# Attention with normalised queries and keys: two key heads per step on the two halves of 64 rows, queries stored without zero padding

## What is computed

```
q, k, v = xq @ wq, xkv @ wk, xkv @ wv      # 16 query heads, 4 key/value heads, 64 channels each
q, k = a * rsqrt(mean(a*a over the 64) + eps) for a in (q, k)
logits = (q @ k.T) / 8                     # each key head serves 4 query heads
out = softmax(logits) @ v @ wo             # added to the residual
```

## Time and profile before

| | |
|---|---|
| median of 3 runs | 2206.13 us |
| lowest, highest | 2204.80, 2211.46 us |
| the profiled execution's own time | 2202.19 us |
| its span | 2200.4 us |
| PE busy | 1836.1 us, 83% |
| DVE busy | 1396.9 us, 63% |
| ACT busy | 877.2 us, 40% |
| mean granted TensorE clock | 0.915 of full |
| `L2_ca` from its first scores to its last projection | about 1129 to 1390 us |
| `L2_sa`, the same | about 1516 to 1667 us |

### The profile page before, as it was taken

The page is one execution under the profiler, slowest core; times in us unless marked ns, Lnnn a source line. Parts: engine busy times, 40 slices in busy tenths (PEclk is TensorE's granted clock), DMA queues, the critical chain, the costliest instruction groups (busy, mean ns, idle before and its releaser), DMA issues.

```text
span 2200.4 us, 34499 instructions
## 1 busy us (share of the span) xinstructions
PE 1836.1 (83%) x10658; PEld 1321.1 (60%) x10658; DVE 1396.9 (63%) x3343; ACT 877.2 (40%) x2513; POOL 640.2 (29%) x710
## 2 busy tenths in 40 slices
PE   5969997399848779998879998877887779988978
PEld 4747775388736567776745554663445655655557
DVE  5856666111168756666756676676777876777765
ACT  4635553122236425554334443333332354444421
POOL 2235553200033335555300000220002243544433
PEclk9979998599969889999879999888998899999979
DMA  4100000388720000010100200110001000001000
GB/s 162 31 19 15 14 0 1 128 272 301 261 101 1 0 8 16 15 45 5 57 15 15 71 0 1 48 58 1 0 0 68 1 11 11 10 10 37 41 1 17
DMA packets 34247, 102.76 MB, mean 47 GB/s; under 512 B 2624, under 2 KB 25696, under 8 KB 26976
## 3 DMA queue, kind: packets, MB, share of 16 engines
q1 hardware_dynamic: 32608, 97.79, 12.9%
q0 software_dynamic: 1536, 3.67, 0.6%
HBM read 93.20 MB, written 8.26 MB: 46 GB/s over the span
## 4 chain that ended last, share of the span: by engine, by line
PE 60%; DVE 18%; issue 10%; ACT 4%; POOL 4%; DMA 3%; DVEq 0%; SPq 0%; POOLq 0%; ACTq 0%
PE ps L750 9%; PE ps L867 7%; PE ps L710 5%; PE ps L715 5%; PE ps L902 4%; PE ps L813 4%; PE ps L763 4%; PE ps L795 4%; PE ps L745 3%; PE ps L997 2%; POOL arena L1734 2%; PE ps L981 2%; DMA arena<-rows_hbm 2%; PE ps L790 2%; PE ps L702 2%
## 5 line engine op out<-in xcount | busy, mean ns | idle before, releaser
L1734 POOL TENSOR_TENSOR arena<-arena,rinv 112x375 f32<-112x375 f32 (+1 forms) x448 | 371.3, 829 | 563.6 <-DVE rinv L1411 555.6
L750 PE MATMUL ps<-arena 128*112 128x375 f32 (+1 forms) x1280 | 387.7, 411 | 20.0 <-ACT arena L1104 13.0
L763 PEld LDWEIGHTS ps<-cst,arena 112*125 112x125 f32 (+1 forms) x1408 | 216.2, 183 | 157.0 <-POOL arena L1734 55.0
L1104 ACT ACTIVATE arena<-ps,negmax 112x375 f32<-112x375 f32 (+1 forms) x384 | 190.2, 500 | 190.9 <-DVE negmax L1406 189.9
L1406 DVE TENSOR_REDUCE negmax<-ps 112x1 f32<-112x375 f32 (+1 forms) x288 | 159.4, 553 | 161.4 <-PE ps L750 161.1
L763 PE MATMUL ps<-cst,arena 112*125 112x112 f32 (+1 forms) x1408 | 229.2, 275 | 38.2 <-POOL arena L1734 37.9
L750 PEld LDWEIGHTS ps<-arena 128*112 128x112 f32 x1280 | 177.3, 183 | 65.7 <-issue 24.6
L1782 POOL TENSOR_TENSOR w_split_sb<-wml,w_split_sb 128x512 fp32r<-128x512 f32 (+1 forms) x40 | 44.8, 1121 | 575.2 <-ACT w_split_sb L1153 573.3
L1104 ACT ACTIVATE arena<-arena,negmax 112x112 f32<-112x112 f32 (+1 forms) x256 | 125.8, 493 | 171.3 <-DVE negmax L1406 171.2
L1420 DVE COPY arena<-ps 125x336 f32<-125x336 f32 x384 | 187.7, 489 | 2.3 <-PE ps L763 1.7
L867 PE MATMUL ps<-h_split_sb,w_split_sb 128*128 128x448 f32 x768 | 178.0, 381 | 8.3 <-DVE h_split_sb L1531 4.3
(11 more groups left out here) (198 smaller groups left out, 3035.8 us busy)
## 6 DMA issues: line engine op xcount, KB each, us to landing
wml<-in_wm_L_moe SPq DMA_DIRECT2D x21, 1028.0 KB, 5.6
wml<-in_wm_L_moe SPq DMA_DIRECT2D x21, 1024.0 KB, 6.1
craw<-in_ctx SPq DMA_DIRECT2D x40, 375.0 KB
wml<-in_wm_L_m SPq DMA_DIRECT2D x3, 3072.0 KB, 12.9
wat<-in_wa_L_ca SPq DMA_DIRECT2D x2, 2560.0 KB, 9.2
wml<-in_wm_L_m SPq DMA_DIRECT2D x2, 2048.0 KB, 9.6
rows_hbm<-wml SPq DMA_DIRECT2D x2, 1344.0 KB, 14.4
arena<-rows_hbm SPq DMA_DIRECT2D x21, 128.0 KB, 5.6
```

The costliest lines, as they stand in the source:

```text
L750: last = mm(ps[0:S, S_BANK + s % blk.s_banks, i * blk.nk:(i + 1) * blk.nk], qz[:, parity(b), head_of(u) if blk.dh == 16 else u], kT[:, par ...
L763: last = nc.tensor.transpose(ps[0:blk.kp, T_BANK + s % blk.t_banks, o:o + S], buf[:, i * blk.nk + q * blk.kp:i * blk.nk + (q + 1) * blk.kp ...
L1104: last = go(probs[0:S, s % blk.nprobs, i * nk:(i + 1) * nk], src[:, i * nk:(i + 1) * nk], ACT.Exp, bias=negmax[:, u:u + 1], accum_out=rows ...
L1734: pool.tensor_tensor(p3, p3, r3, ALU.mult).then_inc(scaled, 1)
```

## The change

In the two blocks a step's scores are no longer issued one by one. At every even step PE issues the scores of steps s and s+1 together: both use only 64 rows, one rows 0 to 63 (`z` = 0) and the other rows 64 to 127 (`z` = 1), into two banks. For that, the steps of `L2_ca` are renumbered: the two heads of a 128-row tile alternate, so that steps 0 to 5 are chunk 0 of heads 0 and 1, chunk 1 of both, chunk 2 of both. `qz` holds the queries once, without zeros, and ACT empties a QT piece in one pass. DVE's additions follow the new numbering. The tables of steps, pieces and banks are the same.

```diff
@@ scores (PE)
+                    n = 2 if blk.pairs else 1
-                    wait(pe, free, count(base, units, b, s - blk.s_banks + 1))
+                    wait(pe, free, count(base, units, b, s + n - blk.s_banks))
...
+                    if blk.pairs:
+                        for z in range(2):
+                            bank = blk.bank_at(s + z)
+                            if blk.keys_first:
+                                g, q = group_of(blk, s + z)
+                                rows = slice(64 * z, 64 * z + 64)
+                                mm(ps[0:blk.kp, bank, 0:HG * S], kT[rows, parity(b), g // 2, q * blk.kp:(q + 1) * blk.kp],
+                                   qz[rows, parity(b), 4 * (g // 2):4 * (g // 2) + 4], start=True, stop=True).then_inc(scored, 1)
...
+                        return
@@ body (PE)
-                        if b != B:
+                        if b != B and (s % 2 == 0 or not blk.pairs):
                             scores(b, s)
@@ piece (ACT)
+                        if blk.pairs:
+                            last = go(qz[:, par, 4 * i:4 * i + 4], W[:, 0:4 * S].rearrange("p (r s) -> p r s", s=S), ACT.Identity, scale=0.125)
-                        for z in range(2):
+                        for z in range(0 if blk.pairs else 2):
@@ exps (ACT), add_chunks (DVE)
-                        g, q = divmod(s, blk.kc)
+                        g, q = group_of(blk, s)
```

More of the change, by code:

```diff
@@ L87 @@
 }
+PAIRS = ("L2_ca", "L2_sa",)
 class Attn:
@@ L109, in __init__ @@
         self.wg = 1 if dh == 16 else 2
+        self.pairs = name in PAIRS
         self.nprobs = 4
@@ L117, in __init__, with bank_at @@
         self.early = [x for s in sorted(self.plan) if s < self.out_step for x in self.plan[s]]
+    def bank_at(self, s):
+        return (s % 3 if s < 14 else 2 * s - 28) if self.s_banks == 3 else s % self.s_banks
     def in_bank(self, bank, before=None):
@@ L485, in head_of, with place, group_of @@
             return 8 * (u // 8) + 2 * (u % 4) + u // 4 % 2
+        def place(blk, u):
+            return 4 * (u // 4) + (0, 2, 1, 3)[u % 4] if blk.pairs and blk.dh == 16 else u
+        def group_of(blk, s):
+            if blk.pairs:
+                return 2 * (s // (2 * blk.kc)) + s % 2, s % (2 * blk.kc) // 2
+            return divmod(s, blk.kc)
         def batches(eng, body):
@@ L742, in scores @@
                         wait_evacuated(pe, blk, st, b, [x for x in blk.pieces if x in ("Q", "Q0", "Q1", "K0", "K1", "QT0", "QT1", "KT0", "KT1")])
+                    if blk.pairs:
[6 more added lines that the diff above has]
+                                   qz[rows, parity(b), 4 * (g // 2):4 * (g // 2) + 4], start=True, stop=True).then_inc(scored, 1)
+                            elif blk.dh == 16:
+                                h = head_of(place(blk, s + z))
+                                rows = slice(64 * z, 64 * z + 64)
+                                mm(ps[0:S, bank, 0:blk.nk], qz[rows, parity(b), 4 * (h // 8) + h % 4],
+                                   kT[rows, parity(b), h // 8, 0:blk.nk], start=True, stop=True).then_inc(scored, 1)
+                            else:
+                                u = s + z
+                                rows = slice(64 * z, 64 * z + 64)
+                                mm(ps[0:S, bank, 0:blk.nk], qz[rows, parity(b), u // 2],
+                                   kT[rows, parity(b), u // 8, 0:blk.nk], start=True, stop=True).then_inc(scored, 1)
+                        return
                     if blk.keys_first:
                         g, q = divmod(s, blk.kc)
-                        mm(ps[0:blk.kp, S_BANK + s % blk.s_banks, 0:HG * S], kT[:, parity(b), g // 2, q * blk.kp:(q + 1) * blk.kp],
+                        mm(ps[0:blk.kp, blk.bank_at(s), 0:HG * S], kT[:, parity(b), g // 2, q * blk.kp:(q + 1) * blk.kp],
                            qz[:, parity(b), HG * g:HG * (g + 1)], start=True, stop=True).then_inc(scored, 1)
@@ L749, in scores @@
                         u = s * blk.heads + i
-                        last = mm(ps[0:S, S_BANK + s % blk.s_banks, i * blk.nk:(i + 1) * blk.nk],
+                        last = mm(ps[0:S, blk.bank_at(s), i * blk.nk:(i + 1) * blk.nk],
                                   qz[:, parity(b), head_of(u) if blk.dh == 16 else u],
@@ L1091, in exps @@
                         act.wait_ge(scored, count(st["unit"], units, b, s + 1))
-                        g, q = divmod(s, blk.kc)
+                        g, q = group_of(blk, s)
                         wait(act, av_done, count(st["group"], 2, b, g // 2 - 1))
-                        go(pT[0:kp, g, q], ps[0:kp, S_BANK + s % blk.s_banks, 0:HG * S].rearrange("p (h s) -> p h s", s=S), ACT.Exp)\
+                        go(pT[0:kp, g, q], ps[0:kp, blk.bank_at(s), 0:HG * S].rearrange("p (h s) -> p h s", s=S), ACT.Exp)\
                             .then_inc(exped, 1)
@@ L1100, in exps @@
                     wait(act, transposed, count(st["turn"], units, b, s - blk.nprobs + 1))
-                    src = ms[0:S, s % 2] if blk.mask else ps[0:S, S_BANK + s % blk.s_banks]
+                    src = ms[0:S, s % 2] if blk.mask else ps[0:S, blk.bank_at(s)]
                     for i in range(blk.heads):
@@ L1391, in maxima @@
                     dve.wait_ge(scored, count(st["unit"], units, b, s + 1))
-                    src = ps[0:S, S_BANK + s % blk.s_banks, 0:blk.heads * nk].rearrange("p (h k) -> p h k", k=nk)
+                    src = ps[0:S, blk.bank_at(s), 0:blk.heads * nk].rearrange("p (h k) -> p h k", k=nk)
                     if blk.mask:
@@ L1419, in copy_turned @@
                     if blk.cross:
-                        last = v.tensor_copy(pT[0:kp, g % 4, :, s % HG], T_[:, 0:KC * S].rearrange("p (k s) -> p k s", s=S))
+                        last = v.tensor_copy(pT[0:kp, g % 4, :, place(blk, s) % HG], T_[:, 0:KC * S].rearrange("p (k s) -> p k s", s=S))
                     else:
```

## The result

The changed kernel takes 2207.86 us (median of 20 runs, 2199.62 to 2220.85), the kernel before 2202.69 us (20 runs, 2194.64 to 2211.46). The ratio is 1.0031, with a 95% interval of 1.0016 to 1.0046: the change costs 0.3%, some 7 us. The three runs known before had a median of 2206.13, 3.4 us above that of the twenty. The two profiled executions took nearly the same (2202.19 before, 2202.40 after), so their spans don't show the loss; their stretches do. Code that is the same in both took 3.8 us less ahead of `L2_ca` and 5.1 us less behind `L2_sa` in the second one. Such stretches scatter: over all profiles of this case, the first query projection of `L2_ca` starts anywhere from 1106.7 to 1121.3 us.

The account below looks back on a forecast made before the run. PE looked like the bound, but DVE's chain was as long in parts of `L2_ca` and bound `L2_sa`. Terms -2.25 (`L2_ca`), -1.95 (`L2_sa`) and +2.8 (clock) gave -1.4 us: 2204.7 us from the 2206.13 median, range 2194 to 2217.

Parts of the forecast that it names:

- The pair's price: Two steps' scores issued together on PE: 0.75 us plus 0.39 for switching to the halved array and back, 1.14 us.
- Rivals 1, 3 and 4: Pair costs 0.75 us (2196 us, chance 0.22); 1.52 us, three slots (2210.5, 0.06); 1.89 us, no overlap (near 2229, 0.10).
- P to T: `L2_ca` batch, from PE finishing QP1 to starting QT0: DVE's chain is as long, so forecast unchanged at 8.98 us.
- T to W: `L2_ca` batch, from QT0's start to weighing the second pair of heads: 6.92 to 6.05 us, then held by DVE.
- W to P: `L2_ca`, from weighing the second pair of heads to the next QP1's end: 15.15 us, set by PE, loses 0.66.
- 0.65 us for KT0: `L2_ca`: PE waits about 0.7 us for ACT to empty KT0 before the next batch's first scores.
- The stretch ahead of each loop: Before the batches of `L2_ca` and `L2_sa`: two of ACT's four QT passes go, -1.05 us in each block.
- `L2_sa`'s weighing: `L2_sa`: starts near 1595.76 instead of 1595.91, held by DVE; -0.15 us in each of six periods, -0.9.
- I count two falls: +2.8: `L2_sa`: PE's clock drops to half twice because its idle stretch gets emptier, at 1.4 us a fall.
- the sum: Whole kernel: -2.25 us for `L2_ca`, -1.95 for `L2_sa`, +2.8 for two clock falls, together -1.4 us.
- Rival 2: `L2_sa`: clock falls in most batches; five falls at 2.2 us are +11, with -4.2 that is 2213 us; chance 0.20.
- the sign named for it: `L2_sa`: a clock of 0.50 in three or more batches would show the forecast wrong.

## Why the prediction was wrong

The time of 2207.86 lies inside the range, but the forecast was 1.4 us less, no change that could be measured, and the change costs 0.3%.

- **The pair's price** was right: 0.75 + 0.39 = 1.14 us forecast, 0.95 + 0.20 = 1.15 measured, with two slots. Rivals 1, 3 and 4 fall.
- **P to T, T to W, W to P** were forecast as 8.98, 6.05 and 15.81 us. They are 1207.21 - 1198.23 = 8.98, 1213.21 - 1207.21 = 6.00 and 30.88 - 14.98 = 15.90. The waits stand where they were said to: DVE's L1406 ahead of QT0, KP1 ahead of `project`, 0.65 us for KT0 where 0.7 was said. `L2_ca` from first scores to last projection was forecast 1.2 us shorter and is 0.7 shorter in the profiles. The stretch ahead of each loop was forecast 1.05 us shorter and is 1.1 and 0.9 shorter.
- **`L2_sa`'s weighing** was forecast 0.15 us earlier, and is.
- **The step that failed** is "I count two falls: +2.8". There are four falls in the five steady periods alone, and they cost (105.7 - 97.0) / 4 = 2.2 us each, where 97.0 is before's 97.75 less the 0.75 forecast: the five periods grew by 7.9 us. All of `L2_sa` from first scores to last projection is 11.7 us longer, where the sum had +1.9 for it. Nothing in the rows supported the number two. I had a warning in the earlier trace rows: the last batch, hardly emptier than a steady one, lost the clock. I took the steady batches' 1.00 as a sign of reserve.
- **Rival 2 happened**, at its own price of 2.2 us a fall, and by the sign named for it (0.50 in three or more batches). Its change, +11 - 4.2 = +6.8 us, is what the ratio gives (0.31% of 2202.69); its 2213 is too high only because it starts from 2206.13. Its reason, and the forecast's, for a fall was the emptier stretch. That is not the whole cause: with each step's scores issued alone the stretch was fuller than before and the clock fell too. What part the scores on half the rows have in it stays open.
- **The absolute time** started from a median of three runs that was 3.4 us too high. That the forecast of 2204.7 lies only 3.2 us from the result is luck: this error and the missing falls have opposite signs.

That matmuls start and end strictly in program order, as the Trainium skill says in "TensorE: Matmul & The Clock Gate", Part 3 (What overlaps and what doesn't), would make a pair 3 x 0.375 + 0.2 = 1.3 us if the rule held for the two records of each matmul, as the prediction read it. The rows show 0.95 on different halves and 1.69 on the same one; neither is 1.3, and on different halves the first records of both matmuls start together, at 1205.22. Whether whole matmuls keep their order the trace can't tell, since its records don't name the half.

## What to carry to other kernels

Before taking work off an engine, ask at each of its waits what the other engines have ready at the time when it would arrive: here six pairs take 6 x (1.50 - 1.15) = 2.1 us off a batch on PE, 1.9 of them were lost to waits, and one moved projection gave them back. Where a change touches PE's idle stretch, by making it emptier or by halving the matmuls in it, read the granted clock of a neighbouring stretch that is nearly as empty; one that has fallen there once is a warning for all of them. Close such a gap by its cause (who is late, and what stands ahead in its list) or fill it; here both brought back about as much.

## What the runs showed of the hardware

- A float32 matmul on half of the rows (64 x 125 weights, 448 columns) takes 0.95 us between starts where a full one takes 0.75, and the full one behind it 0.2 us more than usual. A second one on the other half is free; a second one on the same half costs 0.74.
- Matmuls that nobody reads, about 0.86 us in one gap and 0.64 us in another (an estimate: four records of 256 and of 192 columns, at 0.375 us for 448), made the kernel about 10 us faster than the same kernel without them; nothing starts earlier within the stretch, the clock is 1.00 instead of 0.90. The same kind of filling in a kernel that keeps its clock changed nothing (0.9996).
- Between QT0 and the weighing of `L2_sa`, with the scores on half the rows one at a time, PE was busy 3.26 of 3.91 us with a longest wait of 0.54, and the clock fell twice in five periods. With full-row scores it was busy 3.08 of 4.57 with a wait of 1.47, and the clock held.
